# A mixer, an MLP and a ternary FFN on one Trainium2 core: first tiles ahead of the norm's weights, the small dt product behind the second input product

## What is computed

```python
def mamba2(x, w_in, conv_w, conv_b, A_log, D, dt_bias, w_out):
    zxbcdt = x @ w_in.T
    z, xs, Bs, Cs, dt = jnp.split(zxbcdt, [D_INNER, D_INNER + D_XB, D_INNER + 2 * D_XB, 2 * D_INNER + 2 * D_XB], axis=-1)
    xBC = silu(causal_conv_4_taps(concat(xs, Bs, Cs), conv_w) + conv_b)
    dt = softplus(dt + dt_bias)
    ...
    Y = Y + D[:, None] * xh
    return (Y.reshape(B, L, D_INNER) * silu(z)) @ w_out.T

h = rmsnorm(hidden_states, ln1_w)
h = hidden_states + mamba2(h, ...)
h2 = rmsnorm(h, ln2_w)
mixer = h + silu(h2 @ gate_w.T) * (h2 @ up_w.T) @ down_w.T
x = layernorm(hidden_states + mixer)
x = layernorm(x + bitlinear(bitlinear(x, w_gate) * bitlinear(x, w_up), w_down))
```

## Time and profile before

| | us |
|---|---|
| median of 3 runs | 486.48 (484.66 to 486.71) |
| profiled execution | 484.75 |
| its span | 482.8 |
| TensorE busy | 463.4 (96%) |
| VectorE, ScalarE, GpSimd busy | 332.8, 260.6, 235.5 |
| first transposed tile on TensorE | 8.00 |
| first matmul of dt, of product 0, of product 2 | 12.72, 14.66, 20.23 |

### The profile page before, as it was taken

The page is one execution under the profiler, slowest core; times in us unless marked ns, Lnnn a source line. Parts: engine busy times, 40 slices in busy tenths (PEclk is TensorE's granted clock), DMA queues, the critical chain, the costliest instruction groups (busy, mean ns, idle before and its releaser), DMA issues.

```text
span 482.8 us, 6374 instructions
## 1 busy us (share of the span) xinstructions
PE 463.4 (96%) x2068; PEld 369.7 (77%) x2068; DVE 332.8 (69%) x579; ACT 260.6 (54%) x508; POOL 235.5 (49%) x285
## 2 busy tenths in 40 slices
PE   7999999998999899999999999999998899999995
PEld 7887777775766678888878888888886688887883
DVE  3673876734577777775798999974775565697274
ACT  4889857776656666564432353322717565658000
POOL 6575554535463487867878200045039166752022
PEclk9999999999999999999999999999999999999999
DMA  7620221012112434524313347520200010000022
GB/s 243 238 88 8 81 88 65 22 31 99 59 54 87 132 102 139 196 98 165 132 43 131 132 130 220 188 74 0 87 1 0 0 45 24 1 0 1 0 88 87
DMA packets 14433, 40.81 MB, mean 85 GB/s; under 512 B 2369, under 2 KB 2369, under 8 KB 14401
## 3 DMA queue, kind: packets, MB, share of 16 engines
q1 hardware_dynamic: 14400, 40.41, 24.9%
HBM read 38.30 MB, written 2.10 MB: 84 GB/s over the span
## 4 chain that ended last, share of the span: by engine, by line
PE 85%; DVE 6%; ACT 5%; issue 3%; POOL 2%; POOLq 0%; DVEq 0%; ACTq 0%
PE psA L1696 7%; PE psA L1698 7%; PE psA L1711 4%; PE psA L1713 4%; PE psA L1702 4%; PE psA L1704 3%; PE psB L1907 3%; PE psB L1906 3%; PE psB L1903 3%; PE psA L1684 2%; PE psA L1689 2%; PE psA L1685 2%; PE psB L2004 2%; PE psB L2003 2%; PE psB L1992 2%
## 5 line engine op out<-in xcount | busy, mean ns | idle before, releaser
L785 POOL TENSOR_SCALAR var<-mv 128x1 f32<-128x1 f32 x16 | 4.5, 279 | 108.7 <-DVE mv L1281 108.7
L847 POOL TENSOR_TENSOR beta<-wsum,beta 128x512 fp32r<-128x512 f32 x28 | 36.3, 1315 | 21.2 <-ACT beta L1049 21.2
L1170 ACT ACTIVATE c<-c 128x512 f32<-128x512 f32 x14 | 8.9, 633 | 47.2 <-DVE c L1503 47.2
L1684 PE MATMUL psA<-xT_h,win_h 128*128 128x512 f32 x80 | 32.6, 407 | 0.0
L1685 PE MATMUL psA<-xT_l,win_h 128*128 128x512 f32 x80 | 31.4, 393 | 0.0
L1403 DVE SCALAR_TENSOR_TENSOR xbc<-psA,convw_sb,xbc 128x511 f32<-128x511 f32 (+2 forms) x36 | 26.9, 747 | 4.5 <-ACT xbc L1107 3.6
L1180 ACT ACTIVATE act_hl<-act 128x512 fp32r<-128x512 f32 x28 | 17.0, 628 | 17.6 <-PE psB L1907 11.3
L973 POOL TENSOR_TENSOR int_l<-int,int_h 128x512 fp32r<-128x512 f32 x11 | 16.7, 1514 | 17.5 <-ACT int_h L1251 17.5
L1696 PE MATMUL psA<-xT_h,beta 128*128 128x512 f32 x56 | 22.4, 400 | 0.3 <-DVE act L1519 0.3
L1698 PE MATMUL psA<-xT_l,beta 128*128 128x512 f32 x56 | 21.9, 392 | 0.0
L1689 PE MATMUL psA<-xT_h,win_l 128*128 128x512 f32 x80 | 21.9, 395 | 0.0
(11 more groups left out here) (318 smaller groups left out, 1601.5 us busy)
## 6 DMA issues: line engine op xcount, KB each, us to landing
raw<-in_f_gu_t SPq DMA_DIRECT2D x22, 512.0 KB, 3.4
raw<-in_w_gu_t SPq DMA_DIRECT2D x14, 512.0 KB, 3.5
raw<-in_f_dn_t SPq DMA_DIRECT2D x10, 512.0 KB, 3.4
raw<-in_w_gu_t SPq DMA_DIRECT2D x14, 256.0 KB, 2.6
raw<-in_w_dn_t SPq DMA_DIRECT2D x7, 512.0 KB, 3.4
raw<-in_w_in_t SPq DMA_DIRECT2D x5, 512.0 KB, 4.0
x<-in_hidden SPq DMA_DIRECT2D x8, 256.0 KB, 5.1
out<-x SPq DMA_DIRECT2D x8, 256.0 KB, 2.0
```

Source lines behind the costliest of these rows:

```text
L847: nc.gpsimd.tensor_tensor(beta[:, f % 2, 1, cols], wsum[:, f % 2, cols], beta[:, f % 2, 0, cols].bitcast(F32), ALU.subtract).then_inc(gb_l ...
L1684: nc.tensor.matmul(ps, sh, mh, start=i == 0, stop=False)
```

## The change

Five edits, all in the first 20 us of the program, besides the diagonal:

- SyncE: tiles 0 to 3 first, then the norm's weights, now stored in DRAM as 128 equal rows (256 KB) rather than one; then input weight tile 0, the six constants, input weight tile 1 and the rest as before.
- The high part of input weight tile 0 is made on ScalarE between the turned tiles 1 and 2; its low part on VectorE keeps its place behind the four turned tiles (the new step "low1").
- prepare and dt move from before product 0 to behind product 1. The diagonal leaves prepare and is made behind product 4.
- Product 0 takes all its high tiles first and only then the low ones.
- Fewer idle transposes: 24, 4, 4, 6.

```diff
-    steps += [("turn1", 0), ("turn1", 1), ("prepare",), ("turn1", 2), ("turn1", 3), load("in", 0)]
-    steps += [("dt", 0), load("in", 1), load("in", 2)]
+    steps += [("turn1", 0), ("turn1", 1), load("in", 0), ("turn1", 2), ("turn1", 3), ("low1",)]
+    steps += [load("in", 1), load("in", 2)]
     for j in range(NX + NZ):
         steps += before + [("inproj", 0, j)]
+        if j == 1:
+            steps += [("prepare",), ("dt", 0)]
         if j in (0, 1):
             steps += [("norm1", NC + 2 * j), ("norm1", NC + 2 * j + 1)]
         if j in (0, 2):
             steps.append(load("in", 3 + j // 2))
...
+        if j == NC:
+            steps.append(("diagonal",))
...
-WARM_UP = 30
-KEEP_WARM = {1: 11, 2: 8, 3: 9}
+WARM_UP = 24
+KEEP_WARM = {1: 4, 2: 4, 3: 6}
...
-            load_x(0)
-            load_x(1)
-            sp.dma_start(ln1_sb[:], ln1_w.to_broadcast([P, D])).then_inc(ln1_loaded, 16)
-            for t in range(2, NC):
+            for t in range(NC):
                 load_x(t)
-            sp.dma_start(wdt_raw[:], w_dt).then_inc(consts_loaded, 16)
...
+            sp.dma_start(ln1_sb[:], ln1_w).then_inc(ln1_loaded, 16)
             for n, (kind, *at) in enumerate(LOADS):
...
+                if n == 0:
+                    sp.dma_start(wdt_raw[:], w_dt).then_inc(consts_loaded, 16)
...
+            def diagonal():
+                pool.wait_ge(consts_loaded, N_CONST)
                 nc.gpsimd.tensor_tensor(heads(diag_d[:]), ident[:].unsqueeze(1).to_broadcast([P, H, P]),
...
-                elif kind == "load" and at[0] in INPROJ[:IN_ON_DVE]:
-                    n = at[0]
+                elif kind == "low1" or kind == "load" and at[0] in INPROJ[1:IN_ON_DVE]:
+                    n = at[0] if at else INPROJ[0]
...
-            def split_product(ps, parts, low_weights):
+            def split_product(ps, parts, low_weights, low_moving=()):
                 for i, (sh, _, mh, ml) in enumerate(parts):
                     nc.tensor.matmul(ps, sh, mh, start=i == 0, stop=False)
+                    if not low_moving:
+                        nc.tensor.matmul(ps, sh, ml, start=False, stop=False)
+                for turned in low_moving:
+                    pe.wait_ge(*freed_b(turned))
+                for sh, _, _, ml in parts if low_moving else ():
                     nc.tensor.matmul(ps, sh, ml, start=False, stop=False)
...
-                    for c in range(NC if j == 0 else 0):
-                        pe.wait_ge(*freed_b(("turn1", NC * b + c)))
+                    turned = [("turn1", NC * b + c) for c in range(NC if j == 0 else 0)]
+                    if turned:
+                        pe.wait_ge(xTh_ready, TURNS.index(turned[-1]) + 1)
...
-        "ln1_w": a["ln1_w"].reshape(1, D),
+        "ln1_w": np.broadcast_to(a["ln1_w"].reshape(1, D), (P, D)),
```

More of the change, by code:

```diff
@@ L761, in _ @@
                 sp.dma_start(raw[:, n % RAW_SLOTS, 0:wide], src[:, 0:wide]).then_inc(raw_loaded[n % RAW_SLOTS], 16)
+                if n == 0:
+                    sp.dma_start(wdt_raw[:], w_dt).then_inc(consts_loaded, 16)
+                    sp.dma_start(convw_sb[:], conv_w).then_inc(consts_loaded, 16)
+                    sp.dma_start(convb_sb[:], conv_b).then_inc(consts_loaded, 16)
+                    sp.dma_start(alog_sb[:], a_log.to_broadcast([P, H])).then_inc(consts_loaded, 16)
+                    sp.dma_start(dtb_sb[:], dt_bias.to_broadcast([P, H])).then_inc(consts_loaded, 16)
+                    sp.dma_start(dskip_sb[:], d_skip.to_broadcast([P, H])).then_inc(consts_loaded, 16)
                 if n == 1:
@@ L905, in _ @@
                     prepare()
+                elif kind == "diagonal":
+                    diagonal()
                 elif kind == "load" and at[0] in INPROJ[IN_ON_DVE:]:
@@ L1797, in _ @@
                     split_product(ps, [(win_h[:, j // 2, cols[k]], win_l[:, j // 2, cols[k]], seq(xT_h, k, b),
-                                        seq(xT_l, k, b)) for k in range(KD)], in_split(j // 2)).then_inc(a_done, 1)
+                                        seq(xT_l, k, b)) for k in range(KD)], in_split(j // 2), turned).then_inc(a_done, 1)
                 elif kind == "chunk":
```

## The result

| | before | changed |
|---|---|---|
| median, us | 486.6 (484.66 to 487.28, 4 runs) | **494.14** (492.2 to 495.25, 4 runs) |
| profiled execution, its span | 484.75, 482.8 | 494.04, 492.2 |
| first matmul of product 0 | 14.66 | 11.90 |
| first matmul of dt | 12.72 | 23.86 |
| first matmul of product 2 | 20.23 | 27.41 |

The ratio is 1.0154, 95% interval 1.0124 to 1.0183: 7.5 us slower. The forecast was 490.3 with a range up to 493.6; the sign was right, the size half of it, and the time lies 0.5 us outside the range. The stop of TensorE that the prediction describes is there, 6.0 us long instead of 5.1, and TensorE's granted clock fell besides.

A forecast was written before the change was run, and what follows sets the result against it. TensorE, 96% busy, was taken to bound the kernel through product 2's end. dt at 22.05 plus 1.94 starts product 2 at 24.0 against 20.23, +3.8; on the median 486.48 that gives 490.3 us, range 487.3 to 493.6.

The forecast's parts named there:

- Rival B: GpSimd's queue: input weights 2 land by 12.4, dt starts at 20.3, +2.0 us, 488.5; chance 0.10.
- rival D: Behind product 2: TensorE finds later slack that absorbs dt's delay, about 486 us; chance 0.05.
- +3.8 at product 2's start: TensorE: product 2 starts at 24.0 against 20.23, because dt waits until 22.05 for its small weights.
- input weights 2 land: Transfers: input weights 2 land at 13.85 instead of 15.3, with bounds 12.4 and 15.3.
- GpSimd's queue, first start to dt's start: GpSimd starts at 15.0, needs 6.78 us, then 0.22 for the small part; dt starts at 22.05.
- dt's first matmul to product 2's: TensorE: dt takes 1.94 us to the next product's first matmul, as before the change.
- product 2's first matmul to its takeover: TensorE to ScalarE: product 2 is taken over 3.0 us after its first matmul.
- Start of the transfers: SyncE's first transfers: the norm's weights, stored as a row per partition, cost 0.66 instead of 2.1 us, winning 1.45.
- Rival C: Transfers: the norm's weights load no faster in the new form, input weights 2 land at 15.3, +5.25, 491.7; chance 0.10.
- The lower bound of 12.4: Input weights 2 land at 12.4 if the constants cost 1 to 1.5 us less backlog in the new place.
- rival A: TensorE's stop before dt also costs the clock, dt and most of product 2 at half pace: +5.5, 492.0; chance 0.33.
- A with late weights: TensorE's stop also costs the clock and input weights land late: up to 493.4 us.

The follow-up runs named there:

- e1: The changed kernel with dt's small weights prepared ahead of input weights 1 and 2, dt itself still behind product 1; 486.3 us median, ratio 1.0004.
- e7: The changed kernel with dt's weights prepared right behind the load of input weights 2, dt still behind product 1; 489.4 us median, ratio 1.0089.
- e4: The changed kernel with the norm's weights read from one row of DRAM again; 494.34 us median, ratio 1.0171.
- e3: The kernel before with only prepare and dt moved behind product 1; 491.48 us median, ratio 1.012.
- e6: The changed kernel with the six constants asked for behind input weights 2 and a ScalarE wait for them; 492.23 us median, ratio 1.0121.
- e2: The changed kernel with 52 idle transposes between product 1 and dt; 492.94 us median, ratio 1.0141.
- e5: The changed kernel with the six constants in their order of before, still behind input weights 0; 492.97 us median, ratio 1.0147.

## Why the prediction was right in direction and too small

**Right.** The place (dt's weights behind two low parts and two reciprocals in GpSimd's queue), the sign and the price of the queue: 6.46 us against 6.78 predicted, with nothing else behind product 2 moving until 374 us. e1 removes the queue and all of the loss; e7 takes one low part and the reciprocals out of it, and the stop shrinks from 6.0 to 1.8 us. Rival B, a short queue because of early weights, and rival D, slack that absorbs the delay, did not happen. Product 0 began after a wait of 0.26 where 0.4 was foreseen, though at 11.90 and not at 11.0, as late as the norm's weights were; whether the shorter runs of idle transposes cost nothing, as said, no run tried apart.

**The terms of the sum that were off**, against the +3.8 at product 2's start; the last two are of the same cause:

| step | predicted | measured | difference |
|---|---|---|---|
| input weights 2 land | 13.85 | 15.87 | +2.0 |
| GpSimd's queue, first start to dt's start | 7.05 | 6.83 | -0.2 |
| dt's first matmul to product 2's | 1.94 | 3.55 | +1.6 |
| product 2's first matmul to its takeover | 3.0 | 3.67 | +0.65 |

Together 4.05, and 3.8 + 4.05 is the 7.85 measured. By this sum either error alone would have left the time inside the range: 492.1 with the late weights, 492.6 with the clock.

The first error is in the step "Start of the transfers": it put the slow stretch of 2.1 us down to the row that is read 128 times, because the norm's weights were what landed at its end. That was an inference from landings. The windows show a dip between 3.5 and 6 us in every kernel, whichever way those weights are read: 119 GB/s before, 131 in the changed kernel, 111 in e4, 160 in e3, 180 in e1, 242 in e6, each in its slowest half microsecond, where the better neighbours have 300 to 400. The repeated row's part in it is about half a microsecond (e4), a third of the 1.45 that were counted on; what makes the rest, no run shows. The norm's weights landed at 7.03, not 6.15, 0.9 of the 2.0. Rival C named this cause. The other half is that the constants were moved at an unchanged price: they stand between input weights 0 and 1 and cost 2.4 us there (e6), about 1.2 more than where low rates of before can be put down to them (108, 49, 204 and 255 GB/s in the four half microseconds from 6.5). The lower bound of 12.4 even allowed for their costing less. e3 shows, though, how little of the result hangs on this: with all transfers as before dt starts at the same moment, so the weights' landing near 15.3 to 15.9 is what the old order gave anyway. The forecast had counted on a gain that did not come.

The second error is the clock, left out of the forecast with 0.42 against 0.33 for rival A. A was right: after a stop of 6.0 us the granted clock fell. It was sized at 1.7 us, from the 3.4 us that the cold start runs slowly. Here the lower level lasted 6.8 us, 5.0 of them on work, and cost 2.3 (e2); in e3, e6 and e7 it lasted 3.4 and cost 1.5. The prediction had no row between a wait of 1.4 us, which kept the clock, and its own 5.1; e7 lost it after 1.83. The Trainium skill's rule ("TensorE: Matmul & The Clock Gate", HAM oscillation) that waits of a few microseconds bring the clock down, by which the prediction's sum would have been 1.7 higher, decided here. The trace agrees with it for the stops of 3.8 to 6.0 us; that 1.83 us can be enough, the rule does not say.

The two errors were given as separate rivals, A and C, 492.0 and 491.7. Both came true at once, and in sum they give 3.8 + 2.0 - 0.2 + 2.3. The range allowed for this (A with late weights) only with the small price of the clock, which is why it ended 0.5 us too low. They are not independent either: later weights make a longer stop, and in the profiled executions the stretch at half clock is 3.4 us after stops of up to 4.35 and 6.8 after stops of 5.23 and more. That is not strict: one execution of e5 (491.69 us, mean clock 0.994) has room for a single stretch of 3.4 in all.

## What to carry to other kernels

When a small step is moved later in a list that several engines share, look at each engine's queue: here 0.2 us of GpSimd behind 6.5 us of its own larger work became a 6 us stop of the engine that sets the end, and preparing the small operand early while using it late costs nothing. A stop of the product engine is priced with its clock: by the runs here, add 1.5 us for a stop of 2 to 4 us and 2.2 to 2.8 for one of 5 to 6, or fill it with idle transposes into a bank that is free at that moment. Which transfer made a slow stretch cannot be told from what landed at its end; compare the rates of the same stretch in another kernel, over all of the stretch and not only in its slowest part.

## What the runs showed of the hardware that was not expected

- A stop of 1.83 us was enough for the granted clock to fall to 1.2 GHz (e7), and the loss, measured from dt's first matmul to product 2's takeover, was 6.48 us against 4.94 at the full level. After stops of 3.8 and 4.35 us it was 6.49 and 6.46, after 5.2 to 6.0 us 7.14 to 7.75.
- The fall does not come at once, nor after a fixed time: 2.4 us after TensorE stopped in e7 and 3.3 to 5.3 us after it in the others. In e7 the clock still read 1.00 when TensorE resumed at 19.88 and fell at 20.4, in e6 at 23.4 after work had resumed at 22.84.
- The slow start is not of one length, and the column of the granted clock does not show it: the first idle transposes take 421 ns each until about 6.5 us before and 418 ns as late as 7.8 us in the changed kernel, whose first eight transposes of tiles then take 1.26 us instead of 1.04, while the windows read 1.00 throughout.
- The spread of 2 us between executions of this kernel comes in steps with the mean granted clock: 0.998 or more 484.4 to 485.7, 0.993 or 0.994 486.2 to 487.2, 0.990 488.4 and 488.5 us.
- Six transfers of 29 KB together hold up the large ones behind them by about 2.4 us (e6), and measurably no less in another order (e5).
- A row of 2 KB read 128 times seems to slow the start of the transfers by about half a microsecond against 128 equal rows, by the estimate under e4.
